# Attention: probabilities times values as 16 block-diagonal float32 products per tile

## The chip, the cores and the metric

One Trainium2 chip, one core used. The time is device microseconds of that core for one execution of the whole kernel; the kernel before has a median of 1298.31 us over 3 runs (1295.48 to 1302.3). The engines are named as in the profile: PE (matrix products), PEld (the loads of PE's stationary operand, which run beside the products), DVE (vector), ACT (activations), POOL (general purpose), SP (issues DMAs).

## The reference

The kernel computes one transformer block: layer norm, an attention with a running memory, a residual, a second layer norm, and a mixture of experts (8 experts, the best 2 per token). There are 8 batches of 1024 tokens with 256 features and 16 heads of 16 features. The attention goes over each batch in 16 segments of 64 tokens. What matters here is the part of a segment that does not use the memory, for each head:

```
scores = jnp.matmul(q, jnp.swapaxes(k, -2, -1)) * inv_sqrt_dk
scores = jnp.where(causal, -jnp.inf, scores)
A_dot = jnp.matmul(jax.nn.softmax(scores, axis=-1), v)
A_s = beta * A_mem + (1.0 - beta) * A_dot
```

Here q, k and v are 64 x 16 for one head, one segment and one batch. The softmax is computed as an exponential, a product with v that has a column of ones beside it (this gives the sum of the exponentials), and a division afterwards.

## The kernel before

A tile is one segment of two batches: 128 tokens, of which lanes 0 to 63 belong to the one batch and lanes 64 to 127 to the other. There are 64 tiles. Each stage of the attention is a small function (`t1`, `proj_qk`, `scores`, `pv` and so on) that waits for the semaphores of the stages that it needs, issues its instructions, and raises its own semaphore. The table `program` gives for every engine a list of (lag, stage), written by hand. Round i of an engine runs every stage of its list in the listed order, each on tile i minus its lag. An engine works through its list strictly in order, so a stage that waits holds up all that stand behind it. The table `BANK_FREE` says whose reading must be over before a PSUM bank is written again. After the attention's rounds comes the expert half, which the change does not touch.

Products of float16 operands are made in three parts (high times high, high times low, low times high), so that they come close to float32. The stages around the change, with the lines under which the profile shows them, are these.

- `scores` (L619) and `row_max` (L626, DVE) find each row's maximum; `max_trans` (L631) transposes it.
- `scores_by_key` (L651, L655) computes the scores again with the keys on the lanes, minus the maximum. `softmax_exp` (L662, ACT) writes the exponentials in float32 to `sc`, 128 x 1024: lanes are the keys of both batches, and the columns are 8 groups of 128, each with two heads of 64 queries.
- `p_high` (L667, ACT) copies them to float16, and `p_rest` (L671, POOL) writes what is left over, also in float16.
- `v_high` (L587, ACT) and `v_rest` (L592, DVE) do the same with v. The tile `vs` holds, for each of 8 pairs of heads, 32 columns of v and one column of ones.
- `pv` (L751, PE) makes 48 products per tile: 8 pairs of heads x 3 parts x 2 batches. The stationary operand is 64 x 128 (64 keys of one batch, two heads of 64 queries), the moving one 64 x 33. The two batches lie on different halves of the lanes and go to different banks, D and E.
- `pv_den` (L758), `pv_scale` (L763) and `pv_dve` (L772, four instructions), all on DVE, multiply the sums by a constant per head, take the reciprocal and scale the results. A product with two heads of queries and two heads of values gives four blocks, of which two are of use. `a_add` (POOL), `a_high` (ACT) and `a_rest` (POOL) go on from there, then `a_trans` (L795, PE) and `w_o` (L807, PE).

On PE the order of a round, as the trace shows it from the product of the values on, is `proj_v` (L566), `proj_qk` (L557), `pv` (L751), `a_trans` (L795), `scores_by_key` (L651, L655), `w_o` (L807), `t1` (L536, L537), `scores` (L619), `update` (L727), `router` (L871), `mem_mm` (L681), `h2_trans` (L860) and `max_trans` (L631). `mem_mm` and `update` are float32 products on a quarter of the array each. On DVE `pv_den`, `pv_scale` and `pv_dve` are followed by `ln2_shift` (L834), `q_rest` (L599) and `sigma` (L606). `update` writes banks B and C, which these two and other stages read. From some round on every third round also turns a part of the experts' weights into two float16 halves, on DVE by L76. During set-up L360 makes float32 products on 8 columns.

Of the kernel before, what the change touches and what calls it, by code (L numbers as in the profile page):

```python
# [7 lines left out]
F16 = mybir.dt.float16  # L8
# [19 lines left out]
VW = 2 * DK + 1  # L28
# [171 lines left out]
def attention(nc, ctx, sb_, sem_, psum, banks, x, cT, wmod, wqT, wkT, wvT, woT, beta, rwT, ident,  # L200
# [14 lines left out]
    inv_om = sb("inv_om", [P, NPAIR])  # L215
# [7 lines left out]
    vs = sb("vs", [P, 4, 2, NPAIR, VW], F16)  # L223
# [86 lines left out]
    def set_up_vector(e):  # L310
# [39 lines left out]
        pair = btile2[:, :].rearrange("p (n two) -> p two n", two=2)  # L350
        for par in range(2):
            rows = slice(par * SEG, (par + 1) * SEG)
            e.tensor_scalar(inv_om[rows, :], pair[rows, par, :], 1.0, 1.0 / A_SCALE, ALU.add, ALU.mult).then_inc(s_gb, 1)
        for j in range(1, NJ):
            modulations(j)
    def set_up_tensor(e):
# [7 lines left out]
        for j in range(NJ):  # L364
# [3 lines left out]
            for n in range(3):  # L368
# [17 lines left out]
    pT = sb("pT", [P, 2, 2, 8, P], F16)  # L386
    rr = sb("rr", [P, 2, 2, NPAIR])
# [15 lines left out]
    names = ("stats aggr eps pow nmr xn lna T1 h1T h1L pqk pv qkh exq rel vhi vlo qlo sig scr mx mTr mTh mTl "  # L403
             "sT exp phi plo memm den rec mV mA vpr skt upm umul madd PV pdn rcp ado aadd ahi alo AT aT Wo "
# [15 lines left out]
             (("vhi", 1), ("vlo", 1), ("vpr", 1),)),  # L420
# [14 lines left out]
        "upm": ((("qlo", -2), ("rel", -2), ("qkh", -2), ("sig", -2), ("vhi", -1), ("vlo", -1), ("vpr", -1),),  # L435
# [1038 lines left out]
```

## Time and profile before

| | value |
|---|---|
| median of 3 runs | 1298.31 us |
| time of the profiled execution | 1297.96 us |
| its span | 1296.1 us |
| PE matmul busy | 1153.3 us (89%) |
| PE weight load busy | 979.7 us (76%) |
| DVE busy | 907.1 us (70%) |
| ACT busy | 708.2 us (55%) |
| POOL busy | 932.3 us (72%) |

The busy times are over the whole span. The attention's rounds lie between about 40 and 650 us and the experts' products from about 717 us to the end. The start of one block of products on PE to the start of the next is what a block costs; the duration that a row gives is longer, since it holds the time until the last result is out.

### The profile page before, as it was taken

What the parts mean: (1) busy time and instruction counts of PE and PEld (TensorE: products, weight loads), DVE (VectorE), ACT (ScalarE), POOL (GpSimd) and SP (SyncE); (2) the same over time, 40 slices, a digit from 0 to 9 for tenths busy, and PEclk for the clock granted to TensorE, in tenths of its full rate; (3) what the DMA queues carried; (4) which work ended last, traced back from release to release, by engine and by line L of the source; (5) the groups of instructions that cost most, each with busy time, mean ns of one, the idle gap of its engine ahead of it and who ended that gap; (6) DMA issues with size and microseconds to landing.
All of it is one profiled execution on the core that took longest, in us unless ns stands there. A gap on an engine that the chain in (4) does not pass through costs nothing. (4 is left out here: it accounts for less than half of the span.)

```text
span 1296.1 us, 53596 instructions
## 1 busy us (share of the span) xinstructions
PE 1153.3 (89%) x19576; PEld 979.7 (76%) x19576; DVE 907.1 (70%) x2489; ACT 708.2 (55%) x1393; POOL 932.3 (72%) x989
## 2 busy tenths in 40 slices
PE   4699999999999989999723799999999999999995
PEld 1477778888777777777513688888888888888884
DVE  3699989999899999999888644444444444444442
ACT  2477888888788888888534233333333333333331
POOL 3269989999899998989831466666666666667653
PEclk8799999999899999999755899999999999999998
DMA  8323444334333333333345698999889898888870
GB/s 224 88 63 82 115 115 118 100 97 120 97 102 112 108 105 106 108 100 104 109 125 167 130 132 138 131 136 135 132 135 134 132 138 138 133 134 138 132 110 1
DMA packets 201704, 153.07 MB, mean 118 GB/s; under 512 B 101658, under 2 KB 179570, under 8 KB 201330
## 3 DMA queue, kind: packets, MB, share of 16 engines
q0 software_dynamic: 32592, 56.75, 28.8%
q1 hardware_dynamic: 160770, 81.89, 25.4%
q10 hardware_dynamic: 8096, 11.01, 3.4%
q8 instruction: 171, 2.80, 1.0%
q14 instruction: 75, 0.61, 0.2%
HBM read 63.58 MB, written 44.04 MB: 83 GB/s over the span
## 5 line engine op out<-in xcount | busy, mean ns | idle before, releaser
L1299 PE MATMUL psum<-xT,xall 128*128 128x256 f16 x3408 | 384.9, 273 | 13.7 <-DMA xT<-grow 13.7
L1299 PEld LDWEIGHTS psum<-xT,xall 128*128 x3408 | 334.1, 98 | 53.3 <-issue 14.0
L1361 POOL DMA_INDIRECT out<-late,sidx x142 | 226.8, 1597 | 165.9 <-DVE late L1350 98.8
L1307 ACT ACTIVATE sg<-psum 128x512 f32<-128x512 f32 x142 | 84.8, 597 | 280.9 <-PE psum L1299 280.9
L1312 DVE SCALAR_TENSOR_TENSOR late<-psum,sg 128x512 f32<-128x512 f32 x142 | 98.1, 691 | 184.2 <-ACT sg L1307 184.2
L1279 POOL DMA_INDIRECT grow<-moe_rows,gidx x142 | 146.3, 1030 | 85.6 <-issue 42.7
L1333 PE MATMUL psum<-w2s,hT 128*128 x1704 | 197.7, 273 | 2.8 <-DVE w2s L1387 2.6
L1333 PEld LDWEIGHTS psum<-w2s,hT 128*128 128x128 f16 x1704 | 166.6, 98 | 22.7 <-issue 3.4
L1323 DVE TENSOR_TENSOR hT<-late,hT 128x512 f16<-128x512 f32 x142 | 98.4, 693 | 98.7 <-ACT hT L1319 98.7
L1319 ACT ACTIVATE hT<-late 128x512 f16<-128x512 f32 x142 | 89.4, 630 | 111.7 <-DVE late L1312 111.0
L671 POOL TENSOR_TENSOR pT<-sc,pT 128x1024 f16<-128x1024 f32 x64 | 136.5, 2133 | 8.7 <-ACT pT L667 8.6
L557 PE MATMUL psum<-h1T,wqkv 128*128 128x128 f16 x1536 | 97.4, 220 | 0.9 <-DVE h1T L549 0.9
L557 PEld LDWEIGHTS psum<-h1T,wqkv 128*128 128x128 f16 x1536 | 91.9, 99 | 2.8 <-DVE h1T L549 1.1
L626 DVE TENSOR_REDUCE mx<-psum 128x16 f32<-128x1024 f32 x64 | 77.9, 1218 | 11.3 <-PE psum L619 10.4
L662 ACT ACTIVATE sc<-psum 128x1024 f32<-128x1024 f32 x64 | 65.6, 1025 | 22.4 <-PE psum L655 22.1
L772 DVE TENSOR_TENSOR att_o<-psum,rr 64x128 f32<-64x128 f32 x256 | 73.9, 289 | 5.0 <-DVE rr L763 0.2
L816 POOL TENSOR_TENSOR xall<-xall,gat 128x256 f32<-128x256 f32 x64 | 46.7, 730 | 39.2 <-DVE gat L813 39.2
L651 PE MATMUL psum<-stk 112*64 112x64 f16 x2048 | 59.2, 201 | 14.4 <-DVE vp L698 10.8
L667 ACT ACTIVATE pT<-sc 128x1024 f16<-128x1024 f32 x64 | 67.7, 1057 | 2.0
L651 PEld LDWEIGHTS psum<-stk 112*64 112x64 f16 x2048 | 44.5, 113 | 29.3 <-issue 17.9
L1350 DVE SCALAR_TENSOR_TENSOR late<-psum,wrow,grow 128x256 f32<-128x256 f32 x142 | 62.0, 477 | 2.2 <-PE psum L1333 2.2
L681 PE MATMUL psum<-mem,sig 64*64 64x68 f32 (+1 forms) x2048 | 59.5, 254 | 2.5 <-DVE sig L606 2.3
(263 smaller groups left out, 2298.2 us busy)
## 6 DMA issues: line engine op xcount, KB each, us to landing
stk<-qk SPq DMA_DIRECT2D x384, 64.0 KB, 2.9
moe_rows<-hrows SPq DMA_DIRECT2D x64, 256.0 KB, 4.1
out<-xall SPq DMA_DIRECT2D x64, 128.0 KB, 2.9
raw<-in_w ACTq DMA_DIRECT2D x26, 256.0 KB, 3.3
xall<-in_x ACTq DMA_DIRECT2D x16, 256.0 KB, 4.0
raw<-in_w SPq DMA_DIRECT2D x8, 512.0 KB, 9.5
xall<-in_x SPq DMA_DIRECT2D x8, 384.0 KB, 8.2
grow<-moe_rows,gidx POOLq DMA_INDIRECT x142
```

Source lines behind the costliest of these rows:

```text
L557: i = k.e.matmul(bkB[:, n * P:(n + 1) * P], wqkv[:, b_, c, n * P:(n + 1) * P], h1T[:, k.b, a, c, :], start=(c == 0 and (a, b_) == PARTS[0] ...
L626: done(k.e.tensor_reduce(mx[:, k.b, :], bkDE.rearrange("p h (n k) -> p (h n) k", k=SEG), axis=X, op=ALU.max, negate=True), "mx")
L651: k.e.matmul(bank[toks, gu * P + m * SEG:gu * P + (m + 1) * SEG], stk[:, k.b, h, 1, gu // 2, toks], stk[:, k.b, h, 0, gu // 2, toks], star ...
L671: done(k.e.tensor_tensor(pT[:, k.b, 1, :, :].rearrange("p n t -> p (n t)"), sc[:, k.b, :], pT[:, k.b, 0, :, :].rearrange("p n t -> p (n t) ...
L1279: k.e.indirect_dma_start(grow[:, k.j, q, :], None, rows_dram, at).then_inc(s_g[k.j], 16)
L1299: i = k.e.matmul(bank[:, n * LONG:(n + 1) * LONG], w13s[:, bass.ds(ex_reg * (G * 4 * I) + ((2 * c + b_) * 2 * I + col), P)], xT[:, k.x, a, ...
L1307: done(k.e.activation(sg[:, half, :], bGate[half][:, :], ACT.Silu, scale=1.0 / W_SCALE), "sg")
L1312: done(k.e.scalar_tensor_tensor(out=hf[:, half, :], in0=bUp[half][:, :], scalar=1.0 / W_SCALE, in1=sg[:, half, :], op0=ALU.mult, op1=ALU.m ...
L1319: done(k.e.activation(h_part(k, half, 0), hf[:, half, :], ACT.Copy), "hhi")
L1323: done(k.e.tensor_tensor(h_part(k, half, 1), hf[:, half, :], h_part(k, half, 0), ALU.subtract), "hlo")
L1333: i = k.e.matmul(bY[k.b][:, q * D:(q + 1) * D], hT[:, k.b, a, n, q * P:(q + 1) * P], w2s[:, b_, bass.ds(ex_reg * (KC * D) + n * D, D)], st ...
L1361: k.e.indirect_dma_start(out_rows, bass.IndirectOffsetOnAxis(ap=sidx[:, n:n + 1], axis=0), yo[:, k.v, q, :], None, bounds_check=B * T - 1, ...
```

## The change

The high and low halves of the probabilities and of the values are gone. `pv` takes the exponentials as they are, in float32, and v in float32. Instead of 48 products it makes 16, one per head. The stationary operand is now 128 x 64: the keys of both batches on all lanes, 64 queries of one head. The moving operand is 128 x 34. It is block-diagonal by batch: lanes 0 to 63 hold the first batch's v and a one in columns 0 to 16 and zeros in columns 17 to 33, lanes 64 to 127 the other way round. Results go to lanes 0 to 63 of banks D and E, for both batches side by side.

`p_high`, `p_rest` and `v_rest` go. `v_high` becomes `v_part` with two ACT instructions, one per half of the lanes. `pv_den` has two DVE instructions, the reciprocal is one on 64 lanes x 32, and `pv_dve` has two instructions on 64 x 256 in place of four on 64 x 128. In the set-up POOL clears the whole of `vs` instead of eight small memsets and DVE writes the ones. The hook `x_load` (a DMA issue on ACT's queue in some rounds) moves from `p_high` to `softmax_exp`. No lag in `program` changes.

```
-VW = 2 * DK + 1
+VW = DK + 1
...
-    vs = sb("vs", [P, 4, 2, NPAIR, VW], F16)
+    vs = sb("vs", [P, 4, H, 2, VW])
...
+        e.memset(vs[:, :, :, :, :], 0.0).then_inc(s_mem, 1)
...
-        for b_ in range(4):
-            e.memset(vs[:, b_, 0, :, 2 * DK:VW], 1.0).then_inc(s_c, 1)
-            e.memset(vs[:, b_, 1, :, 2 * DK:VW], 0.0).then_inc(s_c, 1)
...
-        pair = btile2[:, :].rearrange("p (n two) -> p two n", two=2)
-        for par in range(2):
-            rows = slice(par * SEG, (par + 1) * SEG)
-            e.tensor_scalar(inv_om[rows, :], pair[rows, par, :], 1.0, 1.0 / A_SCALE, ALU.add, ALU.mult).then_inc(s_gb, 1)
+        e.tensor_scalar(inv_om[:, :], btile2[:, :], 1.0, 1.0 / A_SCALE, ALU.add, ALU.mult).then_inc(s_gb, 1)
+        e.wait_ge(s_mem, 2)
+        for b2, toks in enumerate(HALVES):
+            e.memset(vs[toks, :, :, b2, DK:VW], 1.0).then_inc(s_c, 1)
...
-    pT = sb("pT", [P, 2, 2, 8, P], F16)
-    rr = sb("rr", [P, 2, 2, NPAIR])
+    rr = sb("rr", [SEG, 2, 2, NPAIR, 2])
...
-    def v_high(k):
+    def v_part(k):
         k.wait("pv")
         k.wait("PV", 4)
-        k.wait("vlo", 4)
-        done(k.e.activation(vs[:, k.j, 0, :, 0:2 * DK], bkC[:, 0:D].rearrange("p (n w) -> p n w", w=2 * DK),
-                            ACT.Copy, scale=1.0 / W_SCALE), "vhi")
-    def v_rest(k):
...
+        for b2, toks in enumerate(HALVES):
+            i = k.e.activation(vs[toks, k.j, :, b2, 0:DK], bkC[toks, 0:D].rearrange("p (h w) -> p h w", w=DK), ACT.Copy,
+                               scale=1.0 / W_SCALE)
+        done(i, "vhi")
...
     def softmax_exp(k):
         k.wait("sT")
-        k.wait("plo", 2)
-        k.wait("phi", 2)
+        k.wait("PV", 2)
...
-    def p_high(k):
...
-    def p_rest(k):
...
     def pv(k):
-        k.wait("plo")
-        k.wait("phi")
-        k.wait("vlo")
+        k.wait("exp")
+        k.wait("vhi")
         k.wait_banks("PV")
-        for half in range(2):
-            for gu in range(4):
-                pair = (gu // 2) * 4 + half * 2 + gu % 2
-                for a, b_ in PARTS:
-                    for r, bank in zip(HALVES, (bkD, bkE)):
-                        i = k.e.matmul(bank[:, pair * VW:(pair + 1) * VW], pT[r, k.b, a, half * 4 + gu, :],
-                                       vs[r, k.j, b_, pair, :], start=((a, b_) == PARTS[0]),
-                                       stop=((a, b_) == PARTS[-1]))
+        for c, bank in enumerate((bkD, bkE)):
+            for n in range(NPAIR):
+                h = c * NPAIR + n
+                half, u, m = n // 4, n // 2 % 2, n % 2
+                at = (half * 4 + c * 2 + u) * P + m * SEG
+                i = k.e.matmul(bank[0:SEG, n * 2 * VW:(n + 1) * 2 * VW], sc[:, k.b, at:at + SEG],
+                               vs[:, k.j, h, :, :].rearrange("p b w -> p (b w)"), start=True, stop=True, skip_group_check=True)
         done(i, "PV")
+    found = bkDE[0:SEG, :, 0:NPAIR * 2 * VW].rearrange("p c (n b w) -> p c n b w", b=2, w=VW)
     def pv_den(k):
...
+        for c in range(2):
+            i = k.e.tensor_tensor(rr[:, k.b, c, :, :], found[:, c, :, :, DK], bc(inv_om[0:SEG, c * NPAIR:(c + 1) * NPAIR], 2),
+                                  ALU.mult)
...
     def pv_dve(k):
...
+        for b2, toks in enumerate(HALVES):
+            i = k.e.tensor_tensor(att_o[toks, k.b, :].rearrange("p (c n w) -> p c n w", c=2, w=DK), found[:, :, :, b2, 0:DK],
+                                  rr[:, k.b, :, :, b2].unsqueeze(3).to_broadcast([SEG, 2, NPAIR, DK]), ALU.mult)
...
-    chunk_work = {p_high: x_load, logit_copy: early_exp, ln2_shift: choice_a, resid: choice_b, var_eps2: choice_c,
+    chunk_work = {softmax_exp: x_load, logit_copy: early_exp, ln2_shift: choice_a, resid: choice_b, var_eps2: choice_c,
```

## Rows read from the trace of the kernel before

**Rows 1.** Windows: stretch, its length, busy us by engine (instructions), PE clock, DMA

```profile
79.70:630.19 550.49, 512.54 (x13268) 425.56 (x13265) 513.00 (x1608) 462.95 (x976) 503.86 (x619) 0.98 0.38 106
206.00:258.00 52.00, 50.63 (x1347) 42.57 (x1344) 50.31 (x164) 46.18 (x99) 49.78 (x63) 1.00 0.34 100
```

**Rows 2.** Timeline of PE: start us, length us, line, operands, idle before

```profile
302.16 1.50 PE L557 MATMUL psum<-h1T,wqkv 128*128 128x128 f16 x24
303.60 0.77 PE L751 MATMUL psum<-vs,pT 64*128 64x33 f16 x48
304.30 0.40 PE L795 MATMUL psum<-idh,ah 128*128 128x128 f16 x4
...
308.29 0.47 PE L727 MATMUL psum<-vp,skt 64*64 64x68 f32 x16 [0.23 <-issue]
...
312.21 0.77 PE L751 MATMUL psum<-vs,pT 64*128 64x33 f16 x48
...
639.72 0.87 PE L751 MATMUL psum<-vs,pT 64*128 64x33 f16 x48 [1.32 <-POOL pT L671]
```

**Rows 3.** Timeline of PE, L631 at both ends of one round

```profile
576.69 0.27 PE L631 MATMUL psum<-idf,mx 128*16 128x128 f32 x1
...
585.12 0.27 PE L631 MATMUL psum<-idf,mx 128*16 128x128 f32 x1
```

**Rows 4.** Source lines on PE: count, ns min/median/max, first to last start us, forms

```profile
L681 PEld LDWEIGHTS psum<-mem,sig x2048: 129/133/228, 50.0 to 620.2; 64*64 64x64 f32 x187
...
L631 PEld LDWEIGHTS psum<-idf,mx x64: 87/90/132, 57.1 to 630.2; 128*16 128x16 f32 x64
L631 PE MATMUL psum<-idf,mx x64: 269/273/418, 57.1 to 630.2; 128*16 128x128 f32 x64
...
L536 PEld LDWEIGHTS psum<-idf,h x128: 137/139/231, 42.3 to 609.4; 128*128 128x128 f32 x128
...
L360 PEld LDWEIGHTS psum<-wmod_sb,cs x12: 86/90/137, 10.8 to 16.7; 128*8 128x8 f32 x12
L360 PE MATMUL psum<-wmod_sb,cs x12: 592/592/1061, 10.8 to 17.1; 128*8 128x512 f32 x12
```

**Rows 5.** Windows of L681: PE matmuls, then PE loads, running in each

```profile
308.92:308.98 0.06, 0.05 (x4) 0.05 (x4) 1.00 0.91 335
308.98:309.04 0.06, 0.06 (x4) 0.06 (x8) 1.00 0.96 359
309.04:309.06 0.02, 0.02 (x8) 0.02 (x12) 1.00 1.08 363
```

**Rows 6.** Timeline of DVE in one round

```profile
302.53 0.32 DVE L696 RECIPROCAL dd<-dd 128x32 f32<-128x32 f32 x1
...
303.97 0.41 DVE L592 SCALAR_TENSOR_TENSOR vs<-psum,vs 128x256 f16<-128x256 f32 x1
304.29 0.41 DVE L713 SCALAR_TENSOR_TENSOR vp<-psum,vp 128x256 f32<-128x256 f32 x1
304.62 0.17 DVE L758 TENSOR_TENSOR rr<-psum,inv_om 128x16 f32<-128x16 f32 x1
304.82 0.25 DVE L763 RECIPROCAL rr<-rr 128x16 f32<-128x16 f32 x1
305.11 1.20 DVE L772 TENSOR_TENSOR att_o<-psum,rr 64x128 f32<-64x128 f32 x4
306.34 0.21 DVE L834 TENSOR_SCALAR nmr<-mv,rstd 128x1 f32<-128x1 f32 x1
```

**Rows 7.** Timeline of ACT and POOL: the instructions that go, and set-up

```profile
307.19 1.06 ACT L667 ACTIVATE pT<-sc 128x1024 f16<-128x1024 f32 x1
...
308.97 2.13 POOL L671 TENSOR_TENSOR pT<-sc,pT 128x1024 f16<-128x1024 f32 x1
...
39.45 1.05 POOL L517 TENSOR_TENSOR rstd<-rstd,mhalf 128x4 f32<-128x4 f32 x1 [27.69 <-ACT nmr L512]
```

**Rows 8.** Source line L76 on DVE, columns as in rows 4

```profile
L76 DVE SCALAR_TENSOR_TENSOR xall<-raw,xall x13: 1418/1477/3069, 338.3 to 658.6; 128x1024 f16<-128x1024 f32 x13
```

More of the change, by code:

```diff
@@ L214, in attention @@
     inv_beta = sb("inv_beta", [P, 2, G, HQ])
-    inv_om = sb("inv_om", [P, NPAIR])
+    inv_om = sb("inv_om", [P, H])
     mhalf = sb("mhalf", [P, 4])
@@ L419, in attention @@
         "pv": ((("umul", 2),),
-             (("vhi", 1), ("vlo", 1), ("vpr", 1),)),
+             (("vhi", 1), ("vpr", 1),)),
         "pqk": ((("umul", 3),),
@@ L434, in attention @@
              (("mTh", 1), ("mTl", 1), ("mx", 1),)),
[L435 removed]
+        "upm": ((("qlo", -2), ("rel", -2), ("qkh", -2), ("sig", -2), ("vhi", -1), ("vpr", -1),),
              (("umul", 1),)),
@@ L659, in softmax_exp @@
         k.wait("sT")
-        k.wait("plo", 2)
-        k.wait("phi", 2)
+        k.wait("PV", 2)
         done(k.e.activation(sc[:, k.b, :], bkFG.rearrange("p h n -> p (h n)"), ACT.Exp, scale=DK ** -0.5), "exp")
-    def p_high(k):
-        k.wait("exp")
-        k.wait("PV", 2)
-        k.wait("plo", 2)
-        done(k.e.activation(pT[:, k.b, 0, :, :].rearrange("p n t -> p (n t)"), sc[:, k.b, :], ACT.Copy), "phi")
-    def p_rest(k):
-        k.wait("phi")
-        k.wait("PV", 2)
-        done(k.e.tensor_tensor(pT[:, k.b, 1, :, :].rearrange("p n t -> p (n t)"), sc[:, k.b, :],
-                               pT[:, k.b, 0, :, :].rearrange("p n t -> p (n t)"), ALU.subtract), "plo")
     def mem_mm(k):
@@ L757, in pv_den @@
         k.wait("ado", 2)
-        done(k.e.tensor_tensor(rr[:, k.b, :, :],
-                               bkDE[:, :, 0:NPAIR * VW].rearrange("p b (n w) -> p b n w", w=VW)[:, :, :, 2 * DK],
-                               bc_mid(inv_om[:, :], 2), ALU.mult), "pdn")
+        for c in range(2):
+            i = k.e.tensor_tensor(rr[:, k.b, c, :, :], found[:, c, :, :, DK], bc(inv_om[0:SEG, c * NPAIR:(c + 1) * NPAIR], 2),
+                                  ALU.mult)
+        done(i, "pdn")
     def pv_scale(k):
         k.wait("pdn")
-        done(k.e.reciprocal(rr[:, k.b, :, :], rr[:, k.b, :, :]), "rcp")
+        flat = rr[:, k.b, :, :, :].rearrange("p c n b -> p (c n b)")
+        done(k.e.reciprocal(flat, flat), "rcp")
     def pv_dve(k):
-        de = [bank[:, 0:NPAIR * VW].rearrange("p (n w) -> p n w", w=VW) for bank in (bkD, bkE)]
         k.wait("rcp")
@@ L768, in pv_dve @@
         k.wait("alo", 2)
-        for b2 in range(2):
-            for par in range(2):
-                r = slice(par * SEG, (par + 1) * SEG)
-                i = k.e.tensor_tensor(
-                    att_o[b2 * SEG:(b2 + 1) * SEG, k.b, :].rearrange(
-                        "p (n w) -> p n w", w=2 * DK)[:, :, par * DK:(par + 1) * DK],
-                    de[b2][r, :, par * DK:(par + 1) * DK], bc(rr[r, k.b, b2, :], DK), ALU.mult)
+        for b2, toks in enumerate(HALVES):
+            i = k.e.tensor_tensor(att_o[toks, k.b, :].rearrange("p (c n w) -> p c n w", c=2, w=DK), found[:, :, :, b2, 0:DK],
+                                  rr[:, k.b, :, :, b2].unsqueeze(3).to_broadcast([SEG, 2, NPAIR, DK]), ALU.mult)
         done(i, "ado")
@@ L886, in attention @@
         "scalar": [(6, qk_high), (6, qk_relu), (10, a_high), (11, a_act), (0, var_eps), (6, qk_exp),
-                  (8, softmax_exp), (8, p_high), (5, h1t), (12, ln2_act), (17, logit_copy), (6, sk_act),
-                  (7, max_high), (13, rows_hi), (3, ln_act), (15, h2_act), (6, v_high)],
-        "gpsimd": [(12, p_rest), (8, ln_mult), (16, ln2_mult), (17, rows_lo), (15, ln2_scale), (12, update_add),
+                  (8, softmax_exp), (5, h1t), (12, ln2_act), (17, logit_copy), (6, sk_act),
+                  (7, max_high), (13, rows_hi), (3, ln_act), (15, h2_act), (6, v_part)],
+        "gpsimd": [(8, ln_mult), (16, ln2_mult), (17, rows_lo), (15, ln2_scale), (12, update_add),
                   (13, a_rest), (16, ln2_add), (3, ln_scale), (12, a_add), (14, res_add), (3, ln_shift)],
```

12 lines of the change are left out of this document (3 added, 9 removed).

## Prediction

> **What bounds the kernel now.** The kernel has two halves, attention and experts, and the page's shares of busy time are means over both. The change lies in the attention half, so I cut that stretch out with the windows view. From 79.70 us to 630.19 us PE is busy 512.54 of 550.49 us, DVE 513.00, POOL 503.86, ACT 462.95 [rows 1]. No engine stands out, so busy time can't say which one sets the pace, and I went on to the timeline of one round. A round treats one tile (128 tokens) in every stage, each stage on another tile, in a fixed order on each engine. L751, the product that is changed, starts at 303.60 and again at 312.21: a round of 8.61 us. In it PE idles 0.23 us, ahead of L727 [rows 2]. In the calm stretch from 206 to 258 us DVE is busy 50.31 of 52.00 us [rows 1]: there DVE is full and PE waits for it a little. PE's own minimum shows in a round without an idle gap on it: L631 starts at 576.69 and at 585.12, so PE's pieces laid end to end take 8.43 us [rows 3]. PE and DVE stand 0.18 us apart, POOL and ACT just behind. L631 runs once per tile, 64 times, the last at 630.2 [rows 4]; from 79.70, where it starts too, there are 60 rounds, on average 550.49 / 60 = 9.17 us. Over PE's 8.43 that is 0.74 us per round: 0.18 for the full DVE, more in the rounds that hold one of 13 large DVE instructions (L76, 1.48 us in the middle, up to 3.07) [rows 8], and irregular waits.
>
> **What the change takes away.** Per tile POOL loses its 2.13 us subtraction L671 and ACT its 1.06 us copy L667 [rows 7]. DVE loses L592, which fills 0.32 us up to the next start (303.97 to 304.29). L772 runs four times on 64x128 and fills 305.11 to 306.34, 1.23 us; two instructions on 64x256 take its place. L592 has the same 256 elements per lane, from PSUM too, and lasts 0.41, so I take 0.42 and 0.35 for the pair: 0.77, a gain of 0.46. The denominators (L758) become two instructions instead of one: it lasts 0.17, and small ones of a pair start about 0.10 apart, so +0.10. The reciprocal goes from 16 to 32 elements, from L763's 0.25 to L696's 0.32: +0.07 [rows 6]. DVE's full round of 8.61 falls by 0.32 + 0.46 - 0.10 - 0.07 = 0.6 us to 8.0. The other end: if each new instruction costs as much as two old ones, the pair gains nothing and DVE's round is 8.5. ACT's copy of v becomes two half-height ones, about 0.3 us more, which the 1.06 us that goes pays for.
>
> **What it adds on PE.** From the start of the old L751 block (48 products) to that of L795 behind it pass 304.30 - 303.60 = 0.70 us [rows 2]. The new block has 16 float32 products: stationary 128 rows x 64 columns (the probabilities of one head, keys of both batches), moving 34 columns. L681 shows how float32 is issued: 16 products per tile, and 2048 loads for 64 tiles, so two loads and two matmuls each [rows 4]. The new block has 32 pairs of load and matmul.
>
> The matmul alone: L360 with 512 float32 columns lasts 592 ns, L631 with 128 lasts 273; (592 - 273) / 384 = 0.83 ns per column [rows 4]. So 34 columns take 28 ns. The old block ran its products two at a time, one on each half of the rows; with some 0.10 us for the change of array shape (an estimate) it made 24 pairs in 0.60 us, 25 ns a pair.
>
> The weight load is the disputed price; no row shows one of 128x64 in float32. The nearest are L681's, 64x64. I cut L681's start in pieces, with the cuts at 308.924, 308.979 and 309.036 (the view rounds them). In the first piece there are four loads and four matmuls, one on each quarter of the array. Four more loads come after 308.979, 55 ns behind the first, and four more matmuls only after 309.036, 57 ns behind these loads [rows 5]. So such a load holds its part of the array for about 55 ns. The durations agree: a 128x16 float32 load lasts 90 ns and a 128x128 one 139 (both feed transposes), (139 - 90) / 112 = 0.44 ns per column; the 64x64 loads last 133, (133 - 90) / 48 = 0.90. [...] So I take 57 ns per record. Low end: 0.44 ns per column, 28 ns, where the matmul with its start sets the step at 31. High end: load and matmul one behind the other, 57 + 30 = 87.
>
> The block is 32 x 57 = 1.82 us, 0.03 for the last matmul, 0.10 for the change of shape: 1.94, or 1.24 more than now. Nothing runs beside anything, as in the old block: all 16 products use all rows and the same 64 columns.
>
> [...]
>
> **What sets the round afterwards.** PE 8.43 + 1.24 = 9.67 us; DVE 8.0; POOL 49.78 / 52 x 8.61 - 2.13 = 6.1; ACT 46.18 / 52 x 8.61 - 0.8 = 6.9 [rows 1]. PE is alone. Is a chain across engines longer than PE's own order? From the end of L751 DVE runs L758, L763, L772, L834, L599 and L606, and L727 on PE, which writes the bank that L606 reads, waits for it. Today the block's results are complete at 303.60 + 0.77 = 304.37 and L727 starts at 308.29, 3.92 later. The edits make this 0.29 shorter (-0.46 + 0.10 + 0.07), and DVE, which now reaches L758 only at 304.62 [rows 6], would be waiting for it and start 0.2 earlier: 3.4. PE's own pieces from that point take 3.92 - 0.23 = 3.69. It just fits, with 0.2 to 0.3 us to spare. The waits that lift today's round get cover: DVE has 9.67 - 8.0 = 1.6 us of slack, more than L76's 1.48. Of the 550.49 - 60 x 8.43 = 44.7 us above PE's minimum, DVE's 0.18 (11 us) and L76 with what follows it (about 21 to 24) go; I keep 10, for waits on DMA and the PE clock lost behind a stall (mean granted clock 0.98 in the stretch).
>
> **The sum.** 60 x 9.67 + 10 = 590 against 550.5: +39.7. The rounds before 79.70 hold two L751 blocks and have idle PE time to give, some 0.9 us each by my reading: 2 x 0.35 = 0.7. At the end the last tile's L751 waits 1.32 us for L671 [rows 2]; 3.2 us of L667 and L671 leave this chain and a block longer by 1.2 us or more (at half clock) comes: -2. Set-up: POOL clears a larger tile, but then idles 27.69 us [rows 7], which hides it; DVE has two small memsets more, under 0.3 us. The x loads move from behind L667 to behind the exponential on ACT's queue, 1.06 us earlier, where nothing waits for them: zero. Expert half: untouched. The profiled execution took 1297.96, so 1297.96 + 38.4 = 1336.4; the median of the runs is 0.35 higher, 1298.31. I say 1337.
>
> **Rivals.**
> (a) Cheap loads, the case on the other side: row halves shared in L681, and a full-height load takes 28 ns. The block is 32 x 31 + 0.13 = 1.12, PE's round 8.85, and with 14 us of waits (DVE is nearer) 60 x 8.85 + 14 = 545: -5.5, with the end's -2 about 1290. The case decides at a step of 36 ns: 32 x 36 + 0.13 - 0.70 = 0.58, a round of 9.01, and 60 x 9.01 + 10 is today's 550.6. [...] 9 in 100.
> [...]
> (b) Serial: 87 ns a record, block 2.91, round 10.64; 60 x 10.64 + 10 = 648, +98; about 1398. 6 in 100.
> (c) The chain from L751 through DVE to L727 becomes the round: if the new DVE instructions cost 0.5 us more than I take, L727 comes 0.3 us late: 60 x 0.3 = +18, 1355. 10 in 100.
> (d) The longer block hides, as if the rounds waited for POOL and ACT all along: about 1298. PE's 0.23 us of idle time in a round speaks against it. 2 in 100.
>
> **Numbers.** The forecast has 73 in 100; its own uncertainty is 55 to 60 ns per load and 4 to 18 us of waits left, 1325 to 1350. With (c) in, 1318 to 1360 leaves out (a), (b), (d) and the tails, 2 in 10. About 0.5% (6.5 us) is what a measurement can tell from no change. Slower 0.90; faster 0.06, most of (a); the same 0.04.
>
> **What will show it.** The new block up to the transposes behind it lasts 1.9 us (1.1 under a, 2.9 under b). Rounds are 9.6 to 9.8 us; DVE waits over 1 us in each for PE, POOL idles some 3, and PE does not idle ahead of L727; if it does, (c) is at work. Waits behind L76 are gone. I am wrong if the rounds stay below 9.2 us.

## The result, and the profile after

The changed kernel takes 1330.41 us (median of 4 runs, 1329.02 to 1334.09) against 1298.64 us for the kernel before on the same chip (4 runs, 1295.48 to 1302.3): a ratio of 1.0251, interval 1.0222 to 1.028. Slower, as predicted (1337, range 1318 to 1360), by 31.8 us instead of 38.7. The profiled execution took 1329.02 us, its span is 1327.2.

The names have new line numbers: `pv` is L731 (L751 before), `proj_qk` L554, `a_trans` L772, `scores` L611, `update` L708 (L727 before), `mem_mm` L662, `max_trans` L623 (L631 before). First the windows view (stretch, its length, busy us by engine, PE clock, DMA), with the same 60 rounds as the first of [rows 1], then the calm stretch:

```profile
84.35:658.97 574.62, 572.43 (x12308) 491.70 (x12305) 478.30 (x1488) 438.79 (x976) 387.36 (x558) 1.00 0.36 101
206.00:258.00 52.00, 52.00 (x1140) 44.56 (x1139) 42.80 (x136) 39.05 (x90) 34.77 (x53) 1.00 0.34 99
```

PE is busy for all of the 52.00 us, DVE no longer is. Per round of 9.60 us that is DVE 7.90, ACT 7.21, POOL 6.42; 8.0, 6.9 and 6.1 were predicted. In the 60 rounds PE idles 574.62 - 572.43 = 2.2 us, against 38 before, at a mean clock of 1.00 against 0.98. The timeline of PE over one round (start us, length us, line, operands, idle before), which answers to [rows 2]:

```profile
305.14 0.27 PE L623 MATMUL psum<-idf,mx 128*16 128x128 f32 x1
...
307.34 2.05 PE L731 MATMUL psum<-vs,sc 128*64 128x34 f32 x32
309.32 0.40 PE L772 MATMUL psum<-idh,ah 128*128 128x128 f16 x4
...
312.39 0.69 PE L611 MATMUL psum<-stk 112*64 112x64 f16 x32
313.02 0.47 PE L708 MATMUL psum<-vp,skt 64*64 64x68 f32 x16
...
314.74 0.27 PE L623 MATMUL psum<-idf,mx 128*16 128x128 f32 x1
```

The reader is to see three things. The block lasts from 307.34 to 309.32, 1.98 us. The round is 314.74 - 305.14 = 9.60 us. And no line has a bracket: the 0.23 us ahead of `update` are gone. Of the 60 rounds 41 take 9.60 us. DVE in the same round, answering to [rows 6]:

```profile
309.43 0.25 DVE L739 TENSOR_TENSOR rr<-psum,inv_om 64x16 f32<-64x16 f32 x2 [1.16 <-PE psum L731]
309.71 0.34 DVE L745 RECIPROCAL rr<-rr 64x32 f32<-64x32 f32 x1
310.09 0.85 DVE L751 TENSOR_TENSOR att_o<-psum,rr 64x256 f32<-64x256 f32 x2
310.97 0.21 DVE L811 TENSOR_SCALAR nmr<-mv,rstd 128x1 f32<-128x1 f32 x1
...
311.70 0.68 DVE L598 SCALAR_TENSOR_TENSOR sig<-psum,ex 128x512 f32<-128x512 f32 x1
```

DVE now stands 1.16 us in front of `pv_den` until the block is done. `sigma` (L598, L606 before) ends at 311.70 + 0.68 = 312.38, and `update` starts at 313.02, 0.64 later. In the kernel before it was less. There `sigma` reads

```profile
307.19 0.68 DVE L606 SCALAR_TENSOR_TENSOR sig<-psum,ex 128x512 f32<-128x512 f32 x1
```

and ends at 307.87, and `update` starts at 308.29 [rows 2], 0.42 later. DVE's wait for `pv` over 80 to 645 us (total, times, longest) and the source lines of `pv`'s loads and of the large instruction L76 (which answers to [rows 8]):

```profile
DVE rr L739 <- PE psum L731: 56.4, 55, 1.4
```
```profile
L731 PEld LDWEIGHTS psum<-vs,sc x2048: 132/138/232, 69.0 to 669.6; 128*64 128x64 f32 x187
...
L76 DVE SCALAR_TENSOR_TENSOR xall<-raw,xall x13: 1215/1217/1606, 364.3 to 687.1; 128x1024 f16<-128x1024 f32 x13
```

### The profile page after: what moved, and what is told of

It is laid out like the page before. It is cut to its first block and busy times, and to the rows that moved or that the text cites. A ratio compares the mean times of both kernels' runs of the same rounds, so it can differ in the third digit from the quotient of the medians.

```text
span 1327.2 us, 51061 instructions
## 1 busy us (share of the span) xinstructions
PE 1223.7 (92%) x18552; PEld 1054.9 (79%) x18552; DVE 873.0 (66%) x2362; ACT 681.3 (51%) x1393; POOL 816.8 (62%) x918
## 5 line engine op out<-in xcount | busy, mean ns | idle before, releaser
L1256 POOL DMA_INDIRECT grow<-moe_rows,gidx x142 | 152.8, 1076 | 85.6 <-issue 42.7
L731 PE MATMUL psum<-vs,sc 128*64 128x34 f32 x2048 | 131.5, 225 | 1.5 <-DVE mTs L632 1.5
L731 PEld LDWEIGHTS psum<-vs,sc 128*64 128x64 f32 x2048 | 124.3, 138 | 8.3 <-issue 1.9
L554 PE MATMUL psum<-h1T,wqkv 128*128 128x128 f16 x1536 | 99.6, 223 | 0.9 <-DVE h1T L546 0.9
L554 PEld LDWEIGHTS psum<-h1T,wqkv 128*128 128x128 f16 x1536 | 93.9, 100 | 3.1 <-DVE h1T L546 1.1
L766 POOL TENSOR_TENSOR ah<-att_o,ah 128x256 f16<-128x256 f32 x64 | 42.9, 670 | 55.4 <-ACT ah L762 54.2
L831 POOL TENSOR_TENSOR hrows<-h,hrows 128x256 f16<-128x256 f32 x64 | 43.1, 674 | 48.9 <-ACT hrows L828 48.9
L757 POOL TENSOR_TENSOR att_o<-att_o,memA 128x256 f32<-128x256 f32 x64 | 46.7, 730 | 31.6 <-DVE att_o L751 31.6
L662 PE MATMUL psum<-mem,sig 64*64 64x68 f32 (+1 forms) x2048 | 58.7, 252 | 3.1 <-DVE sig L598 3.1
```

Source lines behind the costliest of these rows:

```text
L554: i = k.e.matmul(bkB[:, n * P:(n + 1) * P], wqkv[:, b_, c, n * P:(n + 1) * P], h1T[:, k.b, a, c, :], start=(c == 0 and (a, b_) == PARTS[0] ...
L731: i = k.e.matmul(bank[0:SEG, n * 2 * VW:(n + 1) * 2 * VW], sc[:, k.b, at:at + SEG], vs[:, k.j, h, :, :].rearrange("p b w -> p (b w)"), sta ...
L1256: k.e.indirect_dma_start(grow[:, k.j, q, :], None, rows_dram, at).then_inc(s_g[k.j], 16)
```

## The experiments

The question behind all of them: the block costs what was forecast, so what in it costs that (the load, the product, or both in a row), is the relief on the other engines worth anything, and can the relief be had without the price? "Mean round" below is the length of 60 rounds over 60, from the fourth `max_trans` to the last, as in the windows above: 9.17 us before, 9.58 after.

**e1_wide: the moving operand is 68 columns instead of 34, the loads stay.**

```
-                i = k.e.matmul(bank[0:SEG, n * 2 * VW:(n + 1) * 2 * VW], sc[:, k.b, at:at + SEG],
-                               vs[:, k.j, h, :, :].rearrange("p b w -> p (b w)"), ...
+                i = k.e.matmul(bank[0:SEG, n * 2 * VW:(n + 2) * 2 * VW], sc[:, k.b, at:at + SEG],
+                               vs[:, k.j, h:h + 2, :, :].rearrange("p h b w -> p (h b w)"), ...
```

> Only the moving operand of the changed product grows, from 34 to 68 columns (the surplus results are overwritten by the next product or never read). In the changed kernel the steps of this block are 58 ns. Theory as predicted: a 64-column float32 load holds the array for 57 ns and hides the matmul; then 68 columns (about 57 ns) still hide under it, the step stays at 58 to 60 ns, the block at 2.0 us, and the time at about 1331 us. Rival: the load takes only some 28 ns, as the transposes' loads, but does not overlap the matmul, so 28 + 30 = 58; then the step is 28 + 59 = 87 ns, the block 2.9 us, and the time 62 x 0.93 = 58 us longer, about 1388 us.

Measured: 1331.62 us (1329.85 to 1334.53), ratio 1.0261, interval 1.0194 to 1.0327; mean round 9.63. PE timeline:

```profile
301.06 2.11 PE L731 MATMUL psum<-vs,sc 128*64 128x68 f32 x32
303.10 0.40 PE L772 MATMUL psum<-idh,ah 128*128 128x128 f16 x4
```

Twice the columns cost 2.04 - 1.98 = 0.06 us per block. At the 0.83 ns per column that L360 and L631 show [rows 4] the product of one record has gone from 28 to 56 ns, and 32 x 28 ns would be 0.9 us if products stood between the loads. They don't: the load alone sets the step (from record to record 58.3 ns in the middle block in the trace after, 59.2 in e1), and a product of 28 or of 56 ns runs beside it. The rival in the forecast above, a load of 28 ns with the product behind it, falls. So does the prediction's (b), load and product one behind the other: that would be 57 + 56 ns a record here, on the same rows and the same columns, and the two overlap.

**e3_float16: the same 16 products in float16** (`sc` and `vs` in float16, without low halves).

```
-    vs = sb("vs", [P, 4, H, 2, VW])
+    vs = sb("vs", [P, 4, H, 2, VW], F16)
-    sc = sb("sc", [P, 2, 8 * P])
+    sc = sb("sc", [P, 2, 8 * P], F16)
```

> Probabilities and values are written in float16 and the 16 products are made once each in float16, without the low halves, so only a part of the precision is computed; shapes and tiles are those of the changed kernel. 16 records in place of 32. If only float32 keeps load and matmul from overlapping, the step is that of the other 64-column float16 loads, 30 to 32 ns, and the block 0.6 us. If one column half used over and over keeps them from overlapping, it is 27 + 16 = 43 ns and the block 0.8 us. In both cases PE's round falls to 8.2 to 8.4 us, near DVE's 8.1, and the time to 1245 to 1260 us.

Measured: 1257.8 us (1255.5 to 1259.05), ratio 0.9687, interval 0.9626 to 0.9748; mean round 8.46. Timeline and source lines:

```profile
301.85 0.68 PE L731 MATMUL psum<-vs,sc 128*64 128x34 f16 x16
302.46 0.40 PE L772 MATMUL psum<-idh,ah 128*128 128x128 f16 x4
```
```profile
L731 PEld LDWEIGHTS psum<-vs,sc x1024: 105/113/158, 71.4 to 600.6; 128*64 128x64 f16 x171
```

Half the records (16), and each takes (0.61 - 0.10) / 16 = 32 ns instead of (1.98 - 0.10) / 32 = 59. (The 0.10 is an estimate of the change of array shape around the block. In the records of the trace before, the old block's pairs start 25 ns apart, and of its 0.70 us 24 x 25 ns leave 0.10; in the same way 1.98 us less 32 x 58.3 ns leave 0.11 in the kernel after, and 0.61 less 16 x 31.6 leave 0.10 in e3. Between the last product of `proj_v` and the first load of `proj_qk`, of one shape, lie 0.002 us in the middle of the 63 tiles before, between `proj_qk` and `pv`, of two shapes, 0.147.) Both factors belong to float32: two records per product, and twice the time per stationary column (59 / 64 = 0.9 ns against 32 / 64 = 0.5). So the block-diagonal form is not what costs; the type is. (This kernel leaves out the low halves, so its 1257.8 us are not a price for the same precision.)

**e2_two_columns: the two halves of the heads on two column halves of the array** (results on lanes 0 to 63 and 64 to 127 of one bank), DVE's work in 128-lane form again.

```
-        for c, bank in enumerate((bkD, bkE)):
-            for n in range(NPAIR):
+        for n in range(NPAIR):
+            for c, rows in enumerate(HALVES):
...
-                i = k.e.matmul(bank[0:SEG, n * 2 * VW:(n + 1) * 2 * VW], sc[:, k.b, at:at + SEG],
+                i = k.e.matmul(bkD[rows, n * 2 * VW:(n + 1) * 2 * VW], sc[:, k.b, at:at + SEG],
```

> The 16 float32 products alternate between two column halves of the array: heads 0 to 7 to lanes 0 to 63, heads 8 to 15 to lanes 64 to 127, all in one bank; DVE scales in four 64x128 instructions again, with one instruction for the denominators. If the two column halves work beside each other at 58 ns each, the block falls from 1.98 to 16 x 0.058 + 0.13 = 1.06 us, PE's round from 9.60 to about 8.7, DVE's is about 8.3, and the time falls by 62 x 0.9 = 56 us to about 1274 us, below the kernel before. Rival: full-height float32 loads and matmuls exclude each other across the columns too, the block stays at 2.0 us, and the time at 1330 us.

Measured: 1284.48 us (1281.89 to 1287.02), ratio 0.9892, interval 0.9829 to 0.9955; mean round 8.86. PE, then DVE:

```profile
306.17 1.13 PE L733 MATMUL psum<-vs,sc 128*64 128x34 f32 x32
307.23 0.40 PE L772 MATMUL psum<-idh,ah 128*128 128x128 f16 x4
310.30 0.69 PE L613 MATMUL psum<-stk 112*64 112x64 f16 x32
311.02 0.47 PE L710 MATMUL psum<-vp,skt 64*64 64x68 f32 x16
```
```profile
307.84 1.19 DVE L751 TENSOR_TENSOR att_o<-psum,rr 64x128 f32<-64x128 f32 x4
309.06 0.21 DVE L811 TENSOR_SCALAR nmr<-mv,rstd 128x1 f32<-128x1 f32 x1
...
309.92 0.68 DVE L600 SCALAR_TENSOR_TENSOR sig<-psum,ex 128x512 f32<-128x512 f32 x1
```

The block falls from 1.98 to 1.06 us with the same 32 records: (1.06 - 0.10) / 16 = 60 ns for a pair, so two column halves at full height run side by side; in the trace's records the two of a pair start 6 or 7 ns apart, and the next pair 58 ns after this one. The time is 10 us above the 1274 expected. The most frequent round is 8.77 (24 of 60), not the 8.68 of PE's pieces. The way from `pv` through DVE to `sigma` now holds `update` back: it starts 0.72 behind the start of `scores` instead of 0.63, and 0.42 after `sigma`'s end at 309.92 + 0.68 = 310.60, against 0.64 in the kernel after. This is rival (c)'s mechanism at a small size. Both ways, DVE's and PE's, begin where the block ends, so its length doesn't matter to their race. What matters is that `pv_dve` fills 309.06 - 307.84 = 1.22 us in four instructions instead of 0.88 in two. With that the way on DVE is longer than PE's pieces by what `update` comes late.

**e8_two_columns_order: the same, with `ln2_shift` (which nothing on PE waits for) behind `sigma`.**

```
-                  (11, pv_scale), (11, pv_dve), (14, ln2_shift), (8, q_rest), (8, sigma), (13, resid),
+                  (11, pv_scale), (11, pv_dve), (8, q_rest), (8, sigma), (14, ln2_shift), (13, resid),
```

> e2_two_columns with one step of DVE moved: ln2_shift (0.24 us) runs behind sigma instead of ahead of q_rest. In e2 the rounds are 8.77 us with no idle PE but only 8.68 us of PE pieces; the memory update on PE starts 0.42 us behind sigma. If that chain (block end, denominators, reciprocal, scaling, ln2_shift, q_rest, sigma, update) is the bound, the round falls to PE's 8.68 us: 60 x 0.09 = 5 us less, about 1279 us. Rival: another wait is behind the 0.09 us; no change, 1284 us.

Measured: 1279.5 us (1277.84 to 1280.71), ratio 0.9829, interval 0.9793 to 0.9865; mean round 8.77, the ordinary one 8.68.

```profile
309.81 0.27 PE L625 MATMUL psum<-idf,mx 128*16 128x128 f32 x1
...
316.14 0.69 PE L613 MATMUL psum<-stk 112*64 112x64 f16 x32
316.78 0.47 PE L710 MATMUL psum<-vp,skt 64*64 64x68 f32 x16
...
318.50 0.27 PE L625 MATMUL psum<-idf,mx 128*16 128x128 f32 x1
```

`update` is back at 0.64 behind `scores`, and `max_trans` comes 318.50 - 309.81 = 8.69 us after the one before. What is left above 8.68 lies mostly in the rounds with L76 (9.20). The intervals of e2 and e8 overlap; it is the rounds of the traces, 8.77 against 8.68, that show the gain.

**e12_thirds: e8, and L76 cut into three parts, one in each round.**

```
-        if n is not None and part == 0:
+        if n is not None:
-            w13_low(e, w13s, raw[:, n % NRAW, :], n).then_inc(s_rlo, 1)
+            cols = slice((0, 344, 684)[part], (344, 684, 1024)[part])
+            ins = e.scalar_tensor_tensor(out=w13_part(w13s, n, 1)[:, cols], in0=raw[:, n % NRAW, cols], ...
```

> e8_two_columns_order with the 1.22 us DVE instruction that splits expert weights in every third round cut in three thirds of about 0.45 us, one in each round. In e8 the rounds with it are 9.20 us, the others 8.68 us. With thirds DVE has about 8.75 us in each of 39 rounds: 13 x 0.52 = 6.8 us go, 39 x 0.07 = 2.7 us come, 4 us less than e8, about 1275 us. Rival: rounds this close to DVE's limit become uneven, as in e9_four_columns_order, and nothing is gained: 1280 us or more.

Measured: 1274.09 us (1271.09 to 1277.42), ratio 0.9804, interval 0.9772 to 0.9837. The 60 rounds and the parts:

```profile
83.59:603.74 520.15, 517.21 (x12308) 436.64 (x12305) 484.37 (x1569) 432.69 (x976) 381.01 (x558) 1.00 0.41 111
```
```profile
L894 DVE SCALAR_TENSOR_TENSOR xall<-raw,xall x39: 501/505/1065, 337.1 to 633.8; 128x340 f16<-128x340 f32 x26, 128x344 f16<-128x344 f32 x13
```

Mean round 8.67. Three parts cost DVE 3 x 0.505 = 1.5 us where one cost 1.2, and still 520.15 against 526.00 in e8 is 5.9 us less: each part fits into DVE's slack of its own round. The intervals of e8 and e12 overlap, so the 5.9 us rest on one trace of each. Against the kernel before the gain is clear: this version keeps the single float32 product per head and beats it by 25 us.

**e7_four_columns and e9_four_columns_order: four column quarters of 32 queries each,** without and with the order of e8.

```
+            for q in range(4):
+                c, rows = q // 2, slice(q * SEG // 2, (q + 1) * SEG // 2)
...
+                at = (half * 4 + c * 2 + u) * P + m * SEG + q % 2 * SEG // 2
+                i = k.e.matmul(bkD[rows, n * 2 * VW:(n + 1) * 2 * VW], sc[:, k.b, at:at + SEG // 2],
```

> As e2_two_columns, but each product is cut in two of 32 stationary columns, so that the four column quarters of the array work beside each other: 32 products, 64 loads of 128x32. If a load costs by its columns (58 ns for 64), one of 32 columns takes 27 to 31 ns, 16 steps of 31 ns make 0.5 us, and only the issue of 64 pairs (12.5 ns each in the kernel before) holds the block at about 0.9 us; PE's round falls from 8.68 to 8.5 us, but the chain from the block through DVE to the memory update (8.77 us in e2) falls by 0.15 too, so about 1275 us. Rival: the step is a fixed price of a float32 record and not of its columns; then the block is 16 x 58 ns again, 1.06 us, and the time 1284 us.

> e7 and the moved step of e8 together. If both reasons hold, PE's 8.5 us are the round outside those with L76: 1268 to 1272 us. If the load has a fixed price, as e8.

Measured: e7 1286.95 us (1282.92 to 1291.1), ratio 0.9892, interval 0.9853 to 0.993; e9 1284.06 us (1281.65 to 1286.64), ratio 0.9869, interval 0.9832 to 0.9906. e7's timeline and source line, then one block of e9:

```profile
306.82 0.77 PE L734 MATMUL psum<-vs,sc 128*32 128x34 f32 x64
307.57 0.38 PE L773 MATMUL psum<-idh,ah 128*128 128x128 f16 x4
```
```profile
L734 PEld LDWEIGHTS psum<-vs,sc x4096: 106/109/162, 69.6 to 625.2; 128*32 128x32 f32 x196
```
```profile
449.29 0.70 PE L734 MATMUL psum<-vs,sc 128*32 128x34 f32 x56
451.69 0.27 PE L734 MATMUL psum<-vs,sc 128*32 128x34 f32 x8 [1.70 <-issue]
```

The block is 0.75 us, 0.31 less than e2's, so a record has no fixed price of 59 ns: a load of 32 columns lasts 109 ns against 138 for 64, (138 - 109) / 32 = 0.9 ns per column. The four quarters together take a step of (0.75 - 0.10) / 16 = 41 ns, more than the 31 that the columns alone would give; whether the issue of 64 pairs, one per 10 ns, makes the rest was not tested.

Both forecasts of the time were missed (1275 and 1268 to 1272), and neither kernel is faster than e8. PE's busy time per round is 8.46 in e9 (8.65 in e8), its mean round 8.84 (8.77). PE idles 23 us in the 60 rounds. The longest of these idle stretches, up to 1.7 us, lie inside a block, as in the rows above: 56 of the 64 products are done, nothing stands in the program between them and the other 8, and PE stops for 1.70 us. No stage can be the cause. In the 60 rounds such stops (over 0.06 us, between two products of one stage, with no wait or other sequencer instruction between them) make up 10.6 us in 19 places in e9 and 12.0 in 21 in e7. The kernel before has them too, 7.8 us in 16 places, and so has e4 below, 6.8 in 16. One in the kernel before:

```profile
81.91 0.54 PE L751 MATMUL psum<-vs,pT 64*128 64x33 f16 x30
82.97 0.40 PE L751 MATMUL psum<-vs,pT 64*128 64x33 f16 x18 [0.52 <-issue]
```

The kernel after and all other experiments have none, but for one of 0.4 us in e8. The kernels that have them are those with the densest work on PE, counted in the profile's product records: 24.1 per us in the kernel before, 25.2 in e4, 26.6 and 26.8 in e7 and e9, against 21.4 in the kernel after and at most 23.7 in the others (e12); 13268 / 550.49, 13269 / 526.12, 12308 / 574.62 and 12308 / 520.15 are in the windows shown for before, e4, after and e12. And all 72 stops of the four end 1.15 to 1.77 us after a 16 KB packet of the DMA queue that the profile calls `instruction` has landed; such packets come every 4.4 to 4.9 us there (median of each trace). For the two stops shown, in e9 and before, the packets landed at 450.27 and 81.63 us, 1.42 and 1.34 before PE went on. What PE waits for is not shown: this is read from the traces' times alone, and no run varies it by itself.

**e4_relief_alone: the kernel before without `p_rest` and `v_rest`;** the 48 products stay and read the high halves of the probabilities in place of the low ones. Against the kernel before:

```
-        k.wait("plo")
-        k.wait("vlo")
-                        i = k.e.matmul(bank[...], pT[r, k.b, a, half * 4 + gu, :],
+                        i = k.e.matmul(bank[...], pT[r, k.b, 0, half * 4 + gu, :],
```

> The kernel before without the low halves of probabilities and values: POOL's 2.13 us and DVE's 0.32 us per tile are gone, and the 48 float16 products stay (those that took a low half take the high one), so PE's work is unchanged and its results lack precision. This is the change's relief without its price. If the relief is worth what I took, PE's 8.43 us become the round with little on top, 60 x 8.5 = 510 us in place of 550 us, and the time is about 1257 us. Rival: the waits of the kernel before come from DMAs and the clock, not from full DVE and POOL; then at most 15 us are gained, 1283 us.

Measured: 1276.32 us (1275.77 to 1279.32), ratio 0.9834, interval 0.9773 to 0.9895. The 60 rounds:

```profile
84.53:610.65 526.12, 503.67 (x13269) 419.84 (x13265) 491.46 (x1548) 459.49 (x976) 384.55 (x558) 1.00 0.39 111
```

The relief by itself is worth 22 us, half of what was expected of it. PE still idles 526.12 - 503.67 = 22 us, and 6.8 of them are the stops inside blocks that e9 showed. The most frequent round is 8.41 (8 of 60). PE and DVE in one of these:

```profile
405.28 0.70 PE L618 MATMUL psum<-stk 112*64 112x64 f16 x32
406.00 0.47 PE L724 MATMUL psum<-vp,skt 64*64 64x68 f32 x16
...
404.90 0.68 DVE L605 SCALAR_TENSOR_TENSOR sig<-psum,ex 128x512 f32<-128x512 f32 x1
```

`update` starts 0.72 behind `scores` and 0.42 behind the end of `sigma` at 405.58, as in e2 and in the ordinary round of the kernel before. So it is the chain over DVE to `update` that sets this round, and not PE's pieces, which would give 8.32 (8.43 less the 0.11 us explained under e5, since `vlo` is gone from the list here too). DVE is 8.19 us busy per round, so an L76 of 1.3 us doesn't fit, and the rounds with it take 9.4.

**e5_work_back: the changed kernel with the removed work issued again** (a copy on ACT, a subtraction on POOL, one on DVE, and the wait of `update` for `vlo`).

```
-        "upm": ((("qlo", -2), ("rel", -2), ("qkh", -2), ("sig", -2), ("vhi", -1), ("vpr", -1),),
+        "upm": ((("qlo", -2), ("rel", -2), ("qkh", -2), ("sig", -2), ("vhi", -1), ("vlo", -1), ("vpr", -1),),
...
+    def p_high(k):
+    def p_rest(k):
```

> The changed kernel with the removed side work put back: ACT copies the exponentials to float16 (1.06 us per tile), POOL subtracts (2.13 us), DVE makes a low half of v (0.33 us); nothing reads the results. If PE alone sets the round, DVE (8.0 + 0.33), POOL (about 8.2) and ACT (about 8) stay under 9.60 us, rounds stay at 9.6 us and the time at 1330 to 1335 us: the relief is worth nothing once PE is this long. Rival: the relief has carried the calm rounds of the changed kernel (no idle PE at all); then irregular waits as before come back, 10 us or more, 1340 us and above.

Measured: 1340.46 us (1339.2 to 1344.98), ratio 1.031, interval 1.026 to 1.036; mean round 9.71, the ordinary one 9.71 too. PE timeline:

```profile
304.89 0.69 PE L613 MATMUL psum<-stk 112*64 112x64 f16 x32
305.63 0.47 PE L724 MATMUL psum<-vp,skt 64*64 64x68 f32 x16
```

The time is the rival's 1340, above the 1330 to 1335 expected, but no irregular waits came back. The timeline shows no idle time of PE in such a round, yet it is 0.11 us longer, and the place is between `scores` and `update`: 0.74 us here, 0.63 in the kernel after. The kernel before has the 0.74 too, in a round without idle time:

```profile
582.66 0.69 PE L619 MATMUL psum<-stk 112*64 112x64 f16 x32
583.40 0.47 PE L727 MATMUL psum<-vp,skt 64*64 64x68 f32 x16
```

There PE works off the waits that `BANK_FREE` puts ahead of `update`, and the change took one semaphore, `vlo`, out of that list. The source views count the wait instructions (of PE's sequencer, under PEld) between the starts of the two lines: five in the round of the kernel before that stands above, then four in the round of the kernel after at 312.39:

```profile
L449 PEldq EVENT_SEMAPHORE  x3: 51/51/51, 582.9 to 583.1; - x3
L67 PEldq EVENT_SEMAPHORE  x1: 51/51/51, 583.2 to 583.2; - x1
L68 PEldq EVENT_SEMAPHORE  x1: 51/51/51, 583.3 to 583.3; - x1
```
```profile
L446 PEldq EVENT_SEMAPHORE  x2: 51/51/51, 312.6 to 312.7; - x2
L67 PEldq EVENT_SEMAPHORE  x1: 51/51/51, 312.8 to 312.8; - x1
L68 PEldq EVENT_SEMAPHORE  x1: 51/51/51, 312.9 to 312.9; - x1
```

In the trace's records they start 0.105 to 0.111 us apart, and none names more than two semaphores: of PE's wait instructions in the kernel before 899 name two and 771 one; of these five, four name two and the first one, and of the four in the kernel after each names two. Two runs test it.

**e10_one_more_wait: the changed kernel with one semaphore more in that list, one that has long been reached.**

```
-        "upm": ((("qlo", -2), ("rel", -2), ("qkh", -2), ("sig", -2), ("vhi", -1), ("vpr", -1),),
+        "upm": ((("qlo", -2), ("rel", -2), ("qkh", -2), ("sig", -2), ("vhi", -1), ("vpr", -1), ("mA", -1),),
```

> The changed kernel with one more semaphore in the waits of the memory update on PE (that of mem_a for the tile whose v_new is waited for anyway; it is always raised before that). PE takes two semaphores per wait instruction, 0.106 us apart, while the 32 products of the scores ahead of it run. The kernel before has five such instructions there, the changed one four, because the wait for the low half of v is gone. If the fifth sticks out behind the products, rounds go from 9.60 to 9.71 us and the time rises by 60 x 0.11 = 6.6 us, to about 1337 us. Rival: a wait for something long done is free; 1330 us.

**e11_work_back_no_wait: e5 without the wait for `vlo`** (one line of e5's diff less).

> e5_work_back (all side work put back, rounds of 9.71 us, 1340 us) without the one wait for the low half of v in the memory update's list; v_new, which follows it on DVE, is waited for already. If the fifth wait instruction made e5's rounds long, they are 9.60 us again and the time 1333 to 1334 us; what is left over 1330 us is the price of the side work in the rounds with L76. Rival: the side work itself made them long; 1340 us.

Measured: e10 1334.34 us (1329.49 to 1340.46), ratio 1.026, interval 1.0227 to 1.0293; e11 1334.9 us (1329.59 to 1337.2), ratio 1.027, interval 1.0236 to 1.0304. PE in e10, then in e11:

```profile
306.88 0.69 PE L611 MATMUL psum<-stk 112*64 112x64 f16 x32
307.62 0.47 PE L708 MATMUL psum<-vp,skt 64*64 64x68 f32 x16
```
```profile
304.98 0.69 PE L613 MATMUL psum<-stk 112*64 112x64 f16 x32
305.61 0.47 PE L724 MATMUL psum<-vp,skt 64*64 64x68 f32 x16
...
307.33 0.27 PE L625 MATMUL psum<-idf,mx 128*16 128x128 f32 x1
...
316.93 0.27 PE L625 MATMUL psum<-idf,mx 128*16 128x128 f32 x1
```

With the wait 0.74 us, five wait instructions and rounds of 9.71, without any other work added; without it 0.63, four and 9.60, with all the work back. In the traces the wait instruction is the cause, and it costs 0.11 us per round. In all 13 traces the last wait instruction starts 0.11 us ahead of `update`, and the shortest way from `scores` to `update` is 0.74 us in the three kernels with five of them in every round (before, e5, e10) and 0.63 in the ten that have four in most rounds (52 of 64 each). So the four that are left probably still set this start; no run takes one more out. The medians are no test of it: the 60 x 0.11 = 6.6 us are no more than the spread of the runs of one kernel, and e10 and e11 overlap. e11 against the kernel after (4.5 us, overlapping ranges; mean round 9.63 against 9.58) says that the 3 us of POOL and ACT work and the small piece of DVE work per tile are hidden behind the long block: at 9.60 us of PE per round their removal brings 577.84 - 574.62 = 3 us in the 60 rounds.

## Why the prediction was right, and where it was not

The mechanism and the sign held. The spans differ by 31.1 us where the sum said 38.4; by its own terms, with the stretches cut at the same `max_trans` in both traces:

| term | predicted | measured |
|---|---|---|
| block of the values' product | 1.94 us | 1.98 |
| rest of PE's round | 7.73 | 9.60 - 1.98 = 7.62 |
| 60 rounds | +39.7 | 574.62 - 550.49 = +24.1 |
| rounds before them | +0.7 | 84.35 - 79.70 = +4.65 |
| last `max_trans` to the first expert product | -2 | 87.15 - 87.43 = -0.3 |
| expert half | 0 | 581.08 - 578.48 = +2.6 |

- **The load of 57 ns.** Right (59 per record with the product hidden): L681's loads, 55 ns apart with the next matmuls 57 ns behind them, pointed to it [rows 5], and L731's, at full height, are 58 ns apart. e1 shows that the load alone sets the step, e3 that float32 doubles it (59 ns against 32). Why it does, no run shows. Rivals (a) and (b) fall, both by the block (1.12 and 2.91 us).
- **PE alone sets the round.** Right: no idle PE, DVE waits 56.4 us for `pv`. DVE's 7.90 us came out near the 8.0 partly by luck: the prediction took 0.6 off a full round of 8.61, but DVE was busy for 50.31 of 52.00 us there, 8.33 per round, and lost 0.43. The reciprocal and the denominators cost DVE 0.09 and 0.08 us more (0.07 and 0.10 predicted), `pv_dve` 0.88 instead of 0.77. L76 became quicker besides, 1217 ns in the middle against 1477 [rows 8].
- **The chain to `update` fits with 0.2 to 0.3 us to spare.** Right: `update` follows `sigma` by 0.64 us, and by 0.42 in e2, in e4 and in the kernel before, where the chain does set the start. So 0.22 us were to spare, and e2 shows what happens without them.
- **"I keep 10, for waits on DMA and the PE clock lost behind a stall."** This is the step that failed, by 11 us: 60 x 9.60 is 576.0, and the rounds took 574.62. PE idles 2.2 us in them, and the last rounds, with fewer stages, are shorter. The 38 us of before were of several kinds. Two of them, over 80 to 630 us (total, times, longest), wait for a full DVE: `update` for `sigma`, mostly with the 0.42 us above, and `scores_by_key` in rounds with L76:

```profile
PE psum L727 <- issue: 14.2, 33, 1.0
PE psum L651 <- DVE vp L698: 10.8, 11, 2.1
```

With 1.7 us of slack on DVE both are gone, but for one wait of 0.7 us. A third, 7.8 us, are the stops inside blocks (see e7 and e9), which no full engine causes and which e4, with all the relief, keeps (6.8); they are gone in the kernel after and also in e5, with the work back, so the longer block removes them and the relief does not. The prediction had no such term. None of the kinds is left over, and the clock stays at 1.00. Before, it was 0.50 in five stretches, 23.9 us in all by the trace's clock records, each of which began during an idle stretch of PE of 1.22 to 2.14 us or at most 1.9 us behind one.
- **PE's other pieces stay 7.73.** Off by 0.11 us per round, 6.6 us in all: the wait instruction, which I had not counted among what the change removes. With the 0.04 us of the block that is -4.2 us over the 60 rounds.
- **"Have idle PE time to give"**, before 79.70. Wrong: the two rounds with a block grew from 7.96 to 8.84 and 8.81. Their idle time stood ahead of `update`, at the end of the chain that starts with the block, so a block that ends later pushes it. It was 0.90 and 0.94 us and is 0.68 and 0.72 now, so only 0.22 each were given. The other 2.9 us came before any `pv`, with PE at half clock for longer in this execution:

```profile
52.00:56.00 4.00, 2.52 (x60) 1.00 0.22 62
```
```profile
52.00:56.00 4.00, 4.00 (x60) 0.62 0.13 34
```

These are windows of PE before and after (length, busy, clock, DMA share, GB/s); 60 records take 4.00 us instead of 2.52. All eleven experiments had their second `max_trans` later than the kernel before, e4 with the old products too (68.87 us against 63.78), and there is one trace of the kernel before. Whether its early clock was chance stays open.
- **The end, -2.** -0.3: the last `pv` no longer waits (1.32 us for POOL before), but the one before it still waits 1.03 us (1.07 before), now for `mTs`, the maximum's chain on DVE, and both blocks are longer. The +2.6 of the expert half has no counterpart in the code; the clock there is 0.98 against 0.99.

The whole, in effects measured apart, each against the kernel before: the relief on POOL, ACT and DVE without the longer block is worth -22 us (e4, which also drops the wait instruction); the longer block with all that work and the wait kept costs +40 (e5), without the wait +35 (e11); and both together cost +32, not the -22 + 40 = +18. The relief is worth much only while DVE holds up PE; behind a block that makes PE clearly the longest it brings 3 us in the 60 rounds, and the wait instruction 6.

## What to carry to other kernels

Price a float32 product on PE with few moving columns by its stationary ones (here 0.9 ns each, twice per product, and 34 as well as 68 moving columns were hidden behind 64 of them: after and e1), and put small stationary operands side by side on the array's column halves (1.98 us became 1.06 in e2) before giving up the idea: the same change is 2.5% slower on one half and 1.1% faster on two (e2), 1.7% with one DVE step moved (e8). When two engines are nearly equally full, look for the chain between them and for the large instruction that doesn't fit, and cut that into a part per round (e12). A PE that stops in the middle of a block waited for no stage here; more and smaller products made that worse (12.0 and 10.6 us in e7 and e9, 7.8 before). And when work is removed, count the waits that go with it.

## What the runs showed that was not expected

- The block on two column halves of 64, at full height, in float32, takes 1.06 us for the 32 records that take 1.98 on one half (L733 in e2, L731 after); on four quarters of 32 it takes 0.75 us for 64 records (L734 in e7).
- A 128 x 64 stationary operand took 59 ns per record in float32 (after) and 32 in float16 (e3), and with 68 moving columns, 56 ns at 0.83 ns each [rows 4], in place of 34 a record took (2.04 - 1.98) / 32 = 2 ns more (e1).
- A wait on PE for a semaphore that had long been reached cost 0.11 us in e10 (0.74 us between `scores` and `update` against 0.63 after), where it made five wait instructions of four, none with more than two semaphores. That one which fills up an instruction is free would follow from this but was not run.
- PE stops for up to 2.1 us in the middle of a block, with no wait in the program, in the four kernels with 24 or more product records per us, each time 1.15 to 1.77 us after a packet of the `instruction` queue has landed.
- DVE's L76, the same instruction on the same data, takes 1.22 to 1.33 us in the middle (median of 13) in the kernels without POOL's subtraction, 1.48 before, and 1.78 in e5 and e11, which have the subtraction too. What slows it was not measured by itself.
